# Fewer groups of the adjacency beside the encoder, and a weight scale spread by a matmul

## The reference, cut to what matters

```python
edge_index = jnp.stack([src, dst])                 # 20000 edges, 1250 nodes
h = relu(layernorm(x))                             # x: 1250 x 1024
h = sigmoid(h @ wenc.T + benc)                     # encoder, 500 features
h2 = h @ conv_weight
agg = segment_sum(h2[src] * edge_weight[:, None], dst)
x = x + (agg + h @ lin_weight.T) @ wdec.T + bdec
h = relu(layernorm(x))
h = h @ W.T + b                                    # 1024 x 1024
out = x + segment_sum(norm[:, None] * h[col], row) # adjacency with loops, scaled by degrees
```

## Time and profile before

| | us |
|---|---|
| median of 3 runs | 455.64 |
| lowest and highest | 454.35, 456.87 |
| profiled execution, whole | 455.52 |
| profiled execution, span | 453.7 |
| TensorE busy in the span | 444.1 (98%) |
| VectorE busy | 301.2 (66%) |
| ScalarE busy | 237.4 (52%) |

### The profile page before, as it was taken

The page is one execution under the profiler, slowest core; times in us unless marked ns, Lnnn a source line. Parts: engine busy times, 40 slices in busy tenths (PEclk is TensorE's granted clock), DMA queues, the critical chain, the costliest instruction groups (busy, mean ns, idle before and its releaser), DMA issues.

```text
span 453.7 us, 8837 instructions
## 1 busy us (share of the span) xinstructions
PE 444.1 (98%) x3202; PEld 332.8 (73%) x3202; DVE 301.2 (66%) x604; ACT 237.4 (52%) x452; POOL 41.3 (9%) x63
## 2 busy tenths in 40 slices
PE   6999998999999999999999999999999999999997
PEld 4999988978775465469888878888889844444454
DVE  5999895976864243864767776938471657567652
ACT  6987996657769552234244444658463622222220
POOL 2611200000000000000000000464600000000000
PEclk9999999999999999999999999999999999999999
DMA  7950958299457899045800006151758004323433
GB/s 288 306 175 2 173 87 145 70 317 317 143 162 138 265 79 325 3 124 186 302 13 1 1 0 228 53 186 46 287 213 293 1 7 167 129 92 140 156 119 111
DMA packets 48399, 66.37 MB, mean 146 GB/s; under 512 B 25793, under 2 KB 35024, under 8 KB 46820
## 3 DMA queue, kind: packets, MB, share of 16 engines
q1 hardware_dynamic: 48036, 65.39, 48.5%
q0 software_dynamic: 320, 0.39, 0.4%
HBM read 43.62 MB, written 16.77 MB: 133 GB/s over the span
## 4 chain that ended last, share of the span: by engine, by line
PE 84%; ACT 4%; DVE 4%; DMA 4%; SPq 2%; issue 1%; ACTq 0%; DVEq 0%
PE bank L1587 21%; PE bank L1588 21%; PE bank L1589 20%; PE bank L1603 19%; DMA benc_c<-benc 3%; PE bank L1712 2%; DMA h16T<-x 1%; SPq L696 1%; PE bank L1714 1%; ACT h0T L1027 1%; ACT stage L1076 1%; ACT h L979 1%; ACT cnt L1073 1%; DVE stats L1190 1%; DVE h0T L1310 1%
## 5 line engine op out<-in xcount | busy, mean ns | idle before, releaser
L1603 PE MATMUL bank<-a,h_hi 128*128 128x256 f16 (+3 forms) x400 | 85.5, 270 | 0.0
L1603 PE MATMUL bank<-a,h_lo 128*128 128x256 f16 (+3 forms) x400 | 85.5, 270 | 0.0
L1587 PE MATMUL bank<-right,left 128*128 128x512 f16 (+1 forms) x148 | 54.4, 367 | 0.0
L1588 PE MATMUL bank<-right,left 128*128 128x512 f16 (+1 forms) x148 | 54.4, 367 | 0.0
L1589 PE MATMUL bank<-right,left 128*128 128x512 f16 (+1 forms) x148 | 54.4, 367 | 0.0
L1152 ACT CAST left<-zs 128x512 f16<-128x512 f32 x35 | 21.5, 617 | 60.3 <-PE bank L1589 60.3
L1572 DVE SCALAR_TENSOR_TENSOR x<-bank,dis_u,x 128x512 f32<-128x512 f32 (+2 forms) x37 | 26.7, 722 | 34.2 <-PE bank L1589 34.2
L1587 PE MATMUL bank<-h0T,we 128*128 128x256 f32 (+3 forms) x144 | 41.4, 287 | 1.0 <-DVE h0T L1308 1.0
L1603 PEld LDWEIGHTS bank<-a,h_hi 128*128 128x128 f16 (+1 forms) x400 | 38.9, 97 | 4.2 <-issue 0.3
L1603 PEld LDWEIGHTS bank<-a,h_lo 128*128 128x128 f16 (+1 forms) x400 | 39.1, 98 | 3.8
L1587 PE MATMUL bank<-unit,g 128*128 128x500 f16 (+3 forms) x120 | 40.8, 340 | 0.0
(11 more groups left out here) (191 smaller groups left out, 978.2 us busy)
## 6 DMA issues: line engine op xcount, KB each, us to landing
whole<-w SPq DMA_DIRECT2D x7, 1024.0 KB, 7.8
adj_scratch<-stage SPq DMA_DIRECT2D x50, 125.0 KB, 3.5
right_scratch<-right SPq DMA_DIRECT2D x5, 1024.0 KB, 4.0
right<-right_scratch SPq DMA_DIRECT2D x5, 1024.0 KB, 4.8
h<-x SPq DMA_DIRECT2D x9, 512.0 KB, 6.7
x<-x SPq DMA_DIRECT2D x9, 512.0 KB, 5.4
out<-x SPq DMA_DIRECT2D x18, 256.0 KB
w_tile<-w SPq DMA_DIRECT2D x8, 512.0 KB, 4.9
```

The costliest lines, as they stand in the source:

```text
L1587: pe.matmul(o, lhs[0], rhs[0], start=first, stop=False, skip_group_check=True)
L1588: pe.matmul(o, lhs[0], rhs[1], start=False, stop=False, skip_group_check=True)
L1603: ins = pe.matmul(o, h1[i][0:n, k, 128 * f:128 * (f + 1)], moving, start=(k == 0 and part == 0 and i == 0), stop=(k == T - 1 and part == p ...
```

## The change

Six things are changed.

- `due(w)` has a bend at window 22: up to it windows come at a lower rate, behind it at a higher one. Beside the encoder stand windows 0 to 22 (before 0 to 25), beside the ten products and the two groups behind them 23 to 49. Products 3, 5 and 8 have three windows behind them.
- The sums of the convolution weights are spread to all partitions by one matmul with the identity (`spread wc`), in a bank of its own in the rotation; the two DMAs, a buffer and a memset on GpSimd go. The scale and the cuts of these weights come earlier: the scale in block 3, the cuts from block 3 to block 4's second group.
- `split 9` and `turn 9` stand directly behind `split 8` and `turn 8`, ahead of windows 9 and 10.
- The encoder's bias is loaded behind the edge weights.
- One of the eight size passes of the last weights moves from the dense products to the second aggregation.
- `bounds` moves there from step 5 to step 7.

The diff, without declarations and the removal of what is no longer used:

```diff
@@ -52,6 +52,7 @@
 FIRST = 6
 AHEAD = 3
 OPEN = 4.0
+SLOW = 22
 PAIR = 2
 IDLE = (20, 4, 4, 4, 2)
 
@@ -182,15 +183,15 @@
     beside = {
         (1, 0): turn(2)[:2] + fourth[1:3] + turn(2)[2:], (1, 1): fourth[3:], (1, 2): [("norm", 6)] + fifth[:1], (1, 3): [("norm", 7), ("split", 6), ("turn", 6)],
         (2, 0): [("split", 7), ("turn", 7)] + fifth[1:], (2, 1): [("size", "wc")], (2, 2): both(turn(3)) + [("norm", 8)],
-        (2, 3): [("norm", 9), ("split", 8), ("turn", 8), ("limits", "out")],
-        (3, 0): [("split", 9), ("turn", 9)], (3, 1): [("limits", "in")], (3, 2): both(turn(4)),
-        (4, 0): [("limits", "scale")], (4, 1): cut_wc[:1], (4, 2): cut_wc[1:3], (4, 3): cut_wc[3:],
+        (2, 3): [("norm", 9), ("split", 8), ("turn", 8), ("split", 9), ("turn", 9), ("spread", "wc")],
+        (3, 0): [("limits", "scale")], (3, 1): cut_wc[:1], (3, 2): both(turn(4)), (3, 3): cut_wc[1:2],
+        (4, 0): cut_wc[2:3], (4, 1): cut_wc[3:],
     }
     for b in range(1, NB):
         for f in range(KF):
             dense += [("e", b, f)] + ([fourth[0], ("edges",)] if (b, f) == (1, 0) else []) + beside.get((b, f), [])
     dense += [("load", "wl")] + [("g", t) for t in range(4)] + mix(cut_wl, [("g", t) for t in range(4, T)]) + opening[:2]
-    for k, s in enumerate([("g", 2), ("g", 4), ("g", 6), ("g", 8), opening[0]]):
+    for k, s in enumerate([("g", 2), ("g", 4), ("g", 6), ("g", 8)]):
         i = dense.index(s) + 1
         dense[i:i] = [("size", "w1", k)] + [("load", "w1", k + 2)]
     i = dense.index(("g", 0)) + 1
@@ -198,8 +199,13 @@
 
 
     def due(w):
-        return w + OPEN * (NW - w) / NW
-
+
+        if w < SLOW:
+            return OPEN + (share - OPEN) * w / SLOW
+        return share + (NW - share) * (w - SLOW) / (NW - SLOW)
+
+    groups = [s[0] for s in dense[dense.index(("edges",)):] if s[0] in ("e", "g", "swl")]
+    share = NW * groups.count("e") / len(groups)
     stream = [(0, ("hot", 0)), (0, ("hot", 1))]
     for w in range(NW):
         stream += [(due(w), ("win", w))]
@@ -240,7 +246,7 @@
         for k in range(T):
             steps += units[k + AHEAD:k + AHEAD + 1]
             steps += [("sk", n, k)]
-            if (n, k) == (1, 5):
+            if (n, k) == (1, 7):
                 steps += [("bounds",)]
             if (n, k) == (NS - 1, 8):
                 steps += [("scales",)]
@@ -251,8 +257,8 @@
                 steps += [("raw", 1), ("degrees",), ("row", "out"), ("flip", T - 3), ("flip", T - 2), ("flip", T - 1)]
             if (n, k) == (1, 0):
                 steps += [("row", "in"), ("load", "wd")]
-            if n == 1 and k in (1, 2, 3):
-                steps += [("size", "w1", KD - 4 + k)] + [("load", "w1", KD - 2 + k)] * (k == 1)
+            if n == 1 and k in (1, 2, 3, 4):
+                steps += [("size", "w1", KD - 5 + k)] + [("load", "w1", KD - 3 + k)] * (k < 3)
             if n and sums and (n, k) != (1, 0):
                 steps += [("rowsum", sums.pop(0))]
             if n == NS - 1 and k % 2 and k > 1:
@@ -330,7 +335,7 @@
             dense = (0, 8)
         if s[0] == "swl":
             bank_for(("s", s[1], s[2]), *dense)
-        elif s[0] in ("t", "e", "g", "z"):
+        elif s[0] in ("t", "e", "g", "z") or s == ("spread", "wc"):
             if not by_dma(s):
                 bank_for(s, *dense)
         elif s[0] == "o":
...
@@ -356,6 +361,8 @@
                     his[g] = len(his)
         elif s[0] == "lo":
             frees[s[1:]] = len(frees)
+        elif s == ("limits", "scale"):
+            frees["spread", "wc"] = len(frees)
 
     nth = {(p, b): p * NB + b for p in range(NP) for b in range(NB)}
     sums = {s: i + 1 for i, s in enumerate([s for s in STEPS if s[0] in ("fold", "sum")])}
@@ -417,7 +424,7 @@
         csum = small("csum", [P, T], F32)
         cb = small("cb", [P, T], F32)
         minus_half = small("minus_half", [P, 2], F32)
-        sizes = small("sizes", [P, 2], F32)
+        sizes = small("sizes", [P, 1], F32)
         ew_sizes = small("ew_sizes", [EP, 1], F32)
         w1_sizes = small("w1_sizes", [P, KD], F32)
         bounds = small("bounds", [P, 2], F32)
@@ -696,12 +699,11 @@
                 sp.dma_start(h0[t][0:tile_rows(t), :], rows(x, t)).then_inc(x_in[t], 16)
                 if t == 1:
                     sp.dma_start(ew_raw[:], nat_w).then_inc(ew_in, 16)
+                    sp.dma_start(benc_c[:], benc).then_inc(benc_in, 16)
                 if t == 3:
                     for i in range(2):
                         ks = slice(KD // 2 * i, KD // 2 * (i + 1))
                         sp.dma_start(cut_of["we"][0][:, ks, :], wenc.rearrange("(k p) f -> p k f", p=P)[:, ks, :]).then_inc(we_in[i], 16)
-            sp.dma_start(benc_c[:], benc).then_inc(benc_in, 16)
-
             for s in STEPS:
                 if s[0] == "win":
                     w = s[1]
@@ -751,13 +753,6 @@
                     sp.wait_ge(bounds_out, 16)
                     sp.dma_start(all_sizes[:].rearrange("p q i -> p (q i)"),
                                  bound_row.rearrange("q i -> (q i)").unsqueeze(0).broadcast_to([P, 2 * P])).then_inc(bounds_in, 16)
-                elif s == ("limits", "out"):
-                    sp.wait_ge(sizes_ready, 1)
-                    sp.dma_start(limit_row, sizes[:]).then_inc(limits_out, 16)
-                elif s == ("limits", "in"):
-                    sp.wait_ge(limits_out, 16)
-                    sp.dma_start(all_sizes[:].rearrange("p q i -> p (q i)"),
-                                 limit_row.rearrange("q i -> (q i)").unsqueeze(0).broadcast_to([P, 2 * P])).then_inc(limits_in, 16)
                 elif s == ("load", "wc"):
                     sp.dma_start(cut_of["wc"][0][:], wconv.rearrange("(k p) f -> p k f", p=P)).then_inc(cut_in["wc"], 16)
                 elif s == ("load", "wl"):
@@ -989,8 +982,7 @@
                     nc.scalar.activation(w1_tile[k % 2][:], w1_tile[k % 2][:], ACT.Abs, accum_out=w1_sizes[:, k:k + 1]).then_inc(w1_sized, 1)
                 elif s == ("size", "wc"):
                     loaded(act, "wc", 0)
-                    act.wait_ge(size_blank, 1)
-                    nc.scalar.activation(wc_abs[:], wc_raw[:], ACT.Abs, accum_out=sizes[:, 0:1]).then_inc(sizes_ready, 1)
+                    nc.scalar.activation(wc_abs[:], wc_raw[:], ACT.Abs, accum_out=sizes[:]).then_inc(sizes_ready, 1)
                 elif s[0] == "degree":
                     k = s[1]
                     act.wait_ge(cnt_ready, NW)
@@ -1324,8 +1316,10 @@
                     v.scalar_tensor_tensor(g_[1][0:n, t, 0:F], bank[banks_of[s]][0:n, 0:F], scale_of[0][0:n, :], g_[0][0:n, t, 0:F],
                                            ALU.mult, ALU.subtract).then_inc(bank_free, 1)
                 elif s == ("limits", "scale"):
-                    dve.wait_ge(limits_in, 16)
-                    link(v.tensor_reduce(limits[:, 0:1], all_limits, AX, ALU.max))
+                    g = ("spread", "wc")
+                    acc_done(dve, g)
+                    v.tensor_reduce(limits[:, 0:1], bank[banks_of[g]][:, 0:P], AX, ALU.max).then_inc(bank_free, 1)
+                    read_done(dve, g)
                     link(v.tensor_scalar(limits[:, 0:1], limits[:, 0:1], float(P), LEAST, ALU.mult, ALU.max))
                     link(v.tensor_scalar(scales[:, 0:1], limits[:, 0:1].bitcast(I32), EXP_MASK, None, ALU.bitwise_and))
                     link(v.tensor_scalar(scales[:, 0:1], scales[:, 0:1], -1.0, float((HALF_EXP + 254) * EXP_ONE), ALU.mult, ALU.add))
@@ -1681,7 +1675,11 @@
             idle(IDLE[3])
 
             for s in STEPS:
-                if s[0] == "spread":
+                if s == ("spread", "wc"):
+                    pe.wait_ge(sizes_ready, 1)
+                    pe.matmul(take(s)[:, 0:P], sizes[:].broadcast_to([P, P]), ident[:], start=True, stop=True,
+                              skip_group_check=True).then_inc(acc_ready, 1)
+                elif s[0] == "spread":
                     pe.wait_ge(ew_sized, 1)
                     pe.wait_ge(idents, 1)
                     pe.matmul(wbank[0][:, 0:EP], ew_sizes[:].broadcast_to([EP, P]), ident[0:EP, 0:EP], start=True, stop=True,
```

More of the change, by code:

```diff
@@ L306, in build @@
     row = nc.dram_tensor("row_scratch", (T, P), F32).ap()
-    limit_row = nc.dram_tensor("limit_scratch", (P, 2), F32).ap()
     kept = nc.dram_tensor("right_scratch", (NK, P, 2, HK, D // 2), F16).ap()
@@ L346, in build @@
                 bank_for((*s, i), *dense)
-        if s[0] in ("t", "e", "g", "z", "s", "p", "o", "edges"):
+        if s[0] in ("t", "e", "g", "z", "s", "p", "o", "edges") or s == ("spread", "wc"):
             parts = 2 if s in HALVED else {"s": KF, "p": 2}.get(s[0])
@@ L523, in build @@
         scale_of = [scales[:, i:i + 1].bitcast(F32) for i in range(2)]
-        all_limits = all_sizes[:].rearrange("p q i -> p (q i)")
         bank = [ctx.enter_context(nc.psum_tensor(f"bank{i}", [128, 512], F32)) for i in range(8)]
@@ L548, in build @@
         g_pad = sem("g_pad")
```

(5 more changed lines are left out.)

## The result

| | us |
|---|---|
| before, median of 4 runs | 455.39 (454.35 to 456.87) |
| changed, median of 4 runs | 458.73 (458.29 to 459.77) |
| ratio | 1.0079, interval 1.0062 to 1.0095 |
| changed, profiled execution | 458.29, span 456.3 |

The forecast was 456.5 and "no change" with 0.67; the kernel became 3.3 us slower by the medians and 2.8 by the two profiled executions. The measured time lies just inside the upper end of the range, 458.8, a bound that had been set by rival B; that is luck. The five old waits went as forecast. The new waits at the triples (three windows behind one product) were larger, and at the last block of the encoder a new wait of 0.4 us was forecast that did not come.

The account below looks back on a forecast made before the run. TensorE bounds the kernel; only its waits before 139 us can change. New waits 4.95 plus spread 0.22, less 3.86 of old waits and 0.3 for the bias, give +1.0 on 455.52: 456.5 us, range 453.6 to 458.8.

Parts of the forecast that it names:

- rival B: Four transposes in a row choke the DMA queue; last block waits 2.7 us instead of 0.4, total 458.8; chance 0.20.
- The five old waits: TensorE's waits over fixed step prices, from 58.05 us to the second product at 93.75, would go: 3.86 us gained.
- the triples: Products 3, 5 and 8: third window waits 0.8 us for ScalarE's copy of the first, 2.4 us in all.
- a new wait of 0.4 us: Encoder's last block: casts held behind window 9's late store; wait of 0 to 0.9 us, 0.4 taken.
- the bound of 3.6: Upper bound in us on the triples' three waits, if ScalarE is 0.4 late each time.
- Window 11: One-hot tiles late because VectorE idles ahead of the second split: new TensorE wait of 1.5 us, bounds 0 and 2.0.
- Block 3's first group: TensorE waits for ScalarE's window copies: 0.44 us, plus 0.21 in the pair of windows, +0.65 together.
- The small DMAs: The two limits' DMAs replaced by the matmul never held TensorE; only the queue's order could gain.
- landed after 5.3 us: Landing time of a store issued right behind a turn, used to put window 9's store at 73.7 us.
- The bias: Bias load from tenth to fifth queue place shortens a TensorE wait at 31.63 us: -0.3, bounds -0.64 to +0.64.
- The moved steps of the aggregation: Size passes and bounds moved within the second aggregation cost 0, at worst 8.3 us for an unhidden load.

Follow-up runs that it names:

- the three later versions of the changed kernel: Changed kernel with one edit each: split 9 and turn 9 put back (457.03 us), cuts of wl moved (457.42), size pass of wc in block 1 (457.94).
- the kernel of the split alone: Kernel before with only split 9 and turn 9 moved directly behind split 8 and turn 8: 458.09 us, 1.0070.
- the kernel of the spread: Kernel before with only the spread by a matmul and the convolution weights' scale and cuts one block earlier: 453.14 us, 0.9965.
- two others (1.0106, 1.0070): Kernel before with only the bend in due(w), 459.45 us; kernel before with only split 9 and turn 9 moved earlier, 458.09 us.

## Why the prediction was wrong

**The step that failed**, in size, is the price of the triples: "The third starts at 94.55: 0.8 us of wait [...] Three times: 2.4". Three waits of 1.06, 1.89 and 0.86, 3.81 in all, stood in its place. The term was priced on ScalarE's copies alone. That price is right where they decide: 4.70 - 3.90 = 0.80 at the first triple in the three later versions of the changed kernel, and 4.69 - 3.90 = 0.79 at the second, once the cuts had moved. At the second the tile of VectorE decided, 1.89, and moving the cuts took 1.10 of it away. At the third both ends fall together: VectorE's tile (123.69 + 0.41) and ScalarE's copy (123.70 + 0.40) are ready at 124.10, so the 0.86 is near the forecast though VectorE is named as releaser. I had asked of each added window only who frees its bank, and not who makes its input and what stands ahead of that on its engine. In the changed kernel's own profile the first triple took 0.26 more than that 0.80 (ScalarE's copy began 0.57 us after its cast there, and 0.29 with the split put back; no row names what held it), and the bound of 3.6 was passed. The lower clock behind such a wait (1.57 us in one profile) came into no term.

**Window 11** was right in mechanism and size: VectorE idle 2.68 us ahead of the second split, 1.60 for TensorE against 1.5. Putting the split back took 1.29 of it away.

**Block 3's first group** was right in mechanism and size (0.68 against 0.65). In the changed kernel ScalarE begins its group at 53.66, 0.19 behind TensorE's end of 53.47, so it is free in time as forecast. Without the pass over the sizes the two groups of ScalarE began no earlier, at 53.76 and 59.96 against 53.66 and 59.86: the pass costs nothing any more, and the wait that is left is for the work between the two.

**The small DMAs.** "What it replaces never held TensorE" was wrong. With the split moved and the limits' DMAs kept, the last block waits 6.28 - 3.62 = 2.66, and ScalarE's row there names a store as what it waits for; with the split moved and the DMAs gone, 0.03. For the same reason the 0.4 at the last block did not come, and rival B is out: its 458.8 is near the measured time by accident. The store that "landed after 5.3 us" had the small store ahead of it as well as a turn; without that one, stores behind four transposes landed after 2.1. The rule of the Trainium skill's "DMA: Bandwidth & Descriptors", section "Queues, rings and completion order", that an increment waits for earlier writes of the same DMA engine fits the stores of 4.7 us behind the small rows. The 2.0 us that the prediction took from the section "Anatomy of one DMA" of the same page of the Trainium skill stand there for DMAs issued by GpSimd; SP's stores behind the four transposes landed after 2.1 us, near it all the same.

**The bias**: the -0.3 isn't borne out. Moved alone it changed nothing (0.9998), and the +0.09 between the two profiled executions can't be put down to it: the wait that it was to win isn't in every execution, and the start of the kernel differs by more than that between executions. One sign of this is the clock: from 11 to 13 us TensorE's granted clock was 0.50 in the profile of the kernel before and 1.00 in that of the changed one.

**The moved steps of the aggregation** cost nothing, as forecast.

**Open.** Why the last block waited 1.19 us in the kernel before: with the bias alone moved, and the same order of steps there, it was 0.67. The small store and its load explain a part, and up to 2.66 in the kernel of the split alone, but put back into the kernel of the spread they bring waits of 0.22 and 0.17 only. The landing of the transposes differs by over 1 us between kernels, for a reason that was not found. How often the clock falls behind the long waits is open too; it did in one of four profiles.

## What to carry to other kernels

Moving small work from one full stage to another is worth nothing unless every engine that serves it has room at that very place. For each item added, follow both sides, who frees its buffer and who makes its input, and read what stands ahead of that on the second engine: an idle gap there that costs nothing today is the next wait. Take small-row DMAs out of a queue that carries something urgent, and try the parts of a change alone: here one part (0.9965) was worth having and two others (1.0106, 1.0070) ate it.

## What was not expected of the hardware

- A store of 128 rows of 8 bytes makes the 125 KB stores behind it in the queue land after 4.7 us; one row of 512 bytes in its place leaves them at 1.8.
- Behind a wait of 1.74 us TensorE's granted clock was 0.67 over one product in one profile (5.10 us in place of 3.53), and 1.00 in three others with a wait of 1.74 to 1.76.
- The start of the kernel differs between executions by more than an edit there was worth: TensorE's first transposes start at 10.87 to 11.51 us in eleven profiles with the same order of loads.
